# The identity and the causal tile of the mask products: fp32r copies in place of bf16 tiles

## The reference, cut to what matters

```python
x = L0_attn_a_x                                   # 2 x 512 tokens x 256
x = x + _L0_attn_a_ref(_layernorm(x), ...)        # block-sparse causal convolution
x = x + _L0_ffn_ref(_layernorm(x), ...)           # shared + 16 routed experts
x = x + _L0_attn_b_ref(_layernorm(x), ...)        # attention, below
x = x + _L0_ffn_ref(_layernorm(x), ...)

# inside _L0_attn_b_ref: 16 query heads of 128 in 4 key/value groups
scores = jnp.einsum('bhtd,bhsd->bhts', q, k) * scale
causal = jnp.tril(jnp.ones((t, t), dtype=bool))
scores = jnp.where(causal, scores, jnp.finfo(scores.dtype).min)
attn = jax.nn.softmax(scores, axis=-1)
out = jnp.einsum('bhts,bhsd->bhtd', attn, v)
```

## Time and profile before

| | |
|---|---|
| median of 3 runs | 873.85 us (873.17 to 874.07) |
| profiled execution, from first to last instruction (span) | 873.0 us |
| profiled execution, time of its own beside the span | not given apart; the fastest of the three runs took 873.17 us |
| TensorE busy (MATMUL) | 865.5 us, 99% |
| VectorE, ScalarE, GpSimd busy | 501.8, 420.0, 320.0 us |
| mask products (L1746) | 96, from 351.2 to 634.1 us of the span |

### The profile page before, as it was taken

The page is one execution under the profiler, slowest core; times in us unless marked ns, Lnnn a source line. Parts: engine busy times, 40 slices in busy tenths (PEclk is TensorE's granted clock), DMA queues, the critical chain, the costliest instruction groups (busy, mean ns, idle before and its releaser), DMA issues.

```text
span 873.0 us, 16737 instructions
## 1 busy us (share of the span) xinstructions
PE 865.5 (99%) x5617; PEld 773.3 (89%) x5620; DVE 501.8 (57%) x1360; ACT 420.0 (48%) x978; POOL 320.0 (37%) x293
## 2 busy tenths in 40 slices
PE   9999999999999999999999999999999999999998
PEld 7999878888888888889989998998997888888887
DVE  4777757333333338887688668768877433333334
ACT  3522416334334344776377557647746433434332
POOL 5211014556555564232121213212112556556552
PEclk9999999999999999999999999999999999999999
DMA  8999312111111102000000100000002111111111
GB/s 338 362 383 391 136 40 77 49 54 36 54 45 45 54 18 76 1 26 21 18 3 21 36 0 24 0 0 1 1 1 73 38 54 39 51 54 36 54 36 49
DMA packets 25554, 61.01 MB, mean 70 GB/s; under 512 B 3298, under 2 KB 10916, under 8 KB 25508
## 3 DMA queue, kind: packets, MB, share of 16 engines
q1 hardware_dynamic: 23204, 47.82, 16.1%
q0 software_dynamic: 2304, 12.58, 3.8%
HBM read 59.35 MB, written 1.05 MB: 69 GB/s over the span
## 4 chain that ended last, share of the span: by engine, by line
PE 93%; DVE 3%; ACT 1%; DMA 1%; issue 1%; POOL 0%; DVEq 0%; ACTq 0%
PE bank L1131 29%; PE bank L1655 25%; PE bank L1144 14%; PE bank L534 7%; PE bank L545 5%; PE bank L1781 4%; PE bank L1721 3%; PE bank L1157 2%; PE bank L1167 2%; DMA cv_shared<-in_wtaps 1%; PE bank L1746 1%; DVE cv_acc L421 1%; PE bank L518 1%; PE bank L1675 1%; PE bank L129 0%
## 5 line engine op out<-in xcount | busy, mean ns | idle before, releaser
L1030 DVE TENSOR_TENSOR f_h<-f_scaled,bank 128x512 f32<-128x512 f32 (+1 forms) x90 | 60.8, 676 | 179.4 <-POOL f_scaled L895 166.9
L812 ACT ACTIVATE f_h_hi<-f_h 128x512 fp32r<-128x512 f32 (+2 forms) x102 | 63.6, 624 | 186.2 <-DVE f_h L1030 186.0
L895 POOL TENSOR_TENSOR f_scaled<-f_act,f_gate_rows 128x512 f32<-128x512 f32 x80 | 102.9, 1287 | 116.3 <-ACT f_act L805 115.9
L1131 PE MATMUL bank<-f_xt_hi,f_w_lo 128*128 128x512 f32 x352 | 138.2, 393 | 0.0
L1131 PE MATMUL bank<-f_xt_hi,f_w_hi 128*128 128x512 f32 x352 | 137.8, 391 | 0.0
L1350 ACT ACTIVATE at_prob<-bank,at_sbias,at_qrs 128x512 f32<-128x512 f32 (+3 forms) x128 | 77.6, 618 | 72.6 <-DVE at_sbias L1542 72.6
L1037 DVE TENSOR_TENSOR f_h_lo<-f_h,f_h_hi 128x512 fp32r<-128x512 f32 (+2 forms) x102 | 71.8, 704 | 70.7 <-ACT f_h_hi L812 70.4
L1131 PE MATMUL bank<-f_xt_lo,f_w_hi 128*128 128x512 f32 x352 | 108.8, 390 | 0.0
L1144 PE MATMUL bank<-f_w_lo,f_h_hi 128*128 128x256 f32 (+1 forms) x352 | 99.6, 283 | 0.0
L1144 PE MATMUL bank<-f_w_hi,f_h_lo 128*128 128x256 f32 (+1 forms) x352 | 99.6, 283 | 0.0
L1144 PE MATMUL bank<-f_w_hi,f_h_hi 128*128 128x256 f32 (+1 forms) x352 | 99.3, 282 | 0.0
(11 more groups left out here) (232 smaller groups left out, 2062.8 us busy)
## 6 DMA issues: line engine op xcount, KB each, us to landing
cv_raw<-in_wconv SPq DMA_DIRECT2D x26, 512.0 KB, 6.7
cv_shared<-in_wtaps POOLq DMA_DIRECT2D x16, 768.0 KB, 7.7
f_wraw<-in_w SPq DMA_DIRECT2D x42, 256.0 KB, 2.6
xn<-in_wconv SPq DMA_DIRECT2D x14, 512.0 KB, 6.5
f_wraw<-in_w SPq DMA_DIRECT2D x42, 128.0 KB, 2.5
at_wraw<-in_wqkv SPq DMA_DIRECT2D x3, 768.0 KB, 4.4
at_oraw<-in_wo SPq DMA_DIRECT2D x4, 512.0 KB, 3.5
X<-in_x_tiles SPq DMA_DIRECT2D x2, 512.0 KB, 8.0
```

The source lines that it names most:

```text
L812: a.activation(h_hi[slot][0:rows, cols], h_f[half][0:rows, cols], ACT.Copy).then_inc(s["h_hi_done"], 1)
L895: g.tensor_tensor(scaled[half][:], act[half][:], gate_rows[:, half * HALF:(half + 1) * HALF], ALU.mult).then_inc(s["scaled_done"], 1)
L1030: v.tensor_tensor(h_f[half][0:rows, cols], src[half][0:rows, cols], pu[half][0:rows, cols], ALU.mult)\
L1131: mm = t.matmul((pg, pu)[gu][half][0:out_rows, :], w, x, start=q == 0, stop=q == 3 * KH - 1)
```

## The change

The bf16 identity is gone. Two new tiles, `ident_r` and `causal_r`, hold fp32r copies of `ident` and `causal`. ScalarE makes them with two activations late in the convolution phase, and TensorE waits once for them at the head of attention. The three mask products of each step use them in place of the bf16 tiles. The first feed-forward phase no longer allocates a semaphore that it did not use.

```diff
@@ conv_phase, scalar
                     round_sums(st, r)
+            for name in ("ident", "causal"):
+                a.activation(pm[f"{name}_r"][:], pm[name][:], ACT.Copy).then_inc(pm["masks_ready"], 1)
             first_weights["round"](a)
@@ conv_phase, gpsimd
             g.memset(pm["ident"][:], 0.0).then_inc(s["const_done"], 1)
-            g.memset(pm["ident_b"][:], 0.0).then_inc(s["const_done"], 1)
             g.memset(pm["causal"][:], 0.0).then_inc(s["const_done"], 1)
...
-            g.wait_ge(s["const_done"], 4)
-            for m in (pm["ident"], pm["ident_b"]):
-                g.affine_select(out=m[:], in_=m[:], compare_op=ALU.not_equal, fill=1.0, base=0,
-                                pattern=[[-1, P]], channel_multiplier=1)
+            g.wait_ge(s["const_done"], 3)
+            g.affine_select(out=pm["ident"][:], in_=pm["ident"][:], compare_op=ALU.not_equal, fill=1.0, base=0,
+                            pattern=[[-1, P]], channel_multiplier=1)
@@ ffn_phase
-            ... "x_added", "out_done")}
+            ... "x_added")
+             + (() if out is None else ("out_done",))}
@@ attention_phase, tensor, scores
-                        t.matmul(dst, pm["ident_b"][:], mask, start=True, stop=False, skip_group_check=True)
+                        t.matmul(dst, pm["ident_r"][:], mask, start=True, stop=False, skip_group_check=True)
...
-                    open_bank(diagonal(3), pm["causal"][:])
+                    open_bank(diagonal(3), pm["causal_r"][:])
...
-                            open_bank(diagonal(2), pm["causal"][:])
+                            open_bank(diagonal(2), pm["causal_r"][:])
...
-                                      pm["causal"][:].unsqueeze(1).to_broadcast([P, 2, P]))
+                                      pm["causal_r"][:].unsqueeze(1).to_broadcast([P, 2, P]))
@@ attention_phase, tensor
             ln["tensor"](t, 0)
+            t.wait_ge(pm["masks_ready"], 2)
             t.wait_ge(s["wkv_lo_done"], 1)
@@ build
-            "ident_b": sb("ident_b", [P, P], BF16),
             "causal": sb("causal", [P, P], BF16),
+            "ident_r": sb("ident_r", [P, P], F32R),
+            "causal_r": sb("causal_r", [P, P], F32R),
...
+        pm["masks_ready"] = cm("masks_ready")
```

More of the change, by code:

```diff
@@ L707, in ffn_phase @@
             "sentinels_ready", "gate_t", "gate_a", "gate_v", "comb_ready", "gate_rows_ready", "gu_ready", "act_done",
-            "last_w_in", "last_hi_done", "last_lo_done", "scaled_done", "h_ready", "h_hi_done", "h_lo_done", "down_done", "y_ready", "x_added", "out_done")}
+            "last_w_in", "last_hi_done", "last_lo_done", "scaled_done", "h_ready", "h_hi_done", "h_lo_done", "down_done", "y_ready", "x_added")
+             + (() if out is None else ("out_done",))}
         s["w13_hi_done"], s["w13_lo_done"] = first_weights["hi_done"], first_weights["lo_done"]
```

## The result

The changed kernel takes 877.58 us (median of five runs, 877.38 to 877.75), the kernel before 873.85 (873.17 to 874.19): 3.7 us more, ratio 1.004 with a 95% interval of 1.0028 to 1.0052. The forecast was 877.2, range 875.8 to 879.0.

The account below looks back on a forecast made before the run. TensorE's loads and products, one after the other, were taken to bound attention. 26 x 0.08 + 32 x 0.04 = 2.1 + 1.3 = 3.4 us on 873.85 gave 877.2 us, range 875.8 to 879.0, chance 0.80.

Parts of the forecast that it names:

- What bounds: Attention steps: TensorE's loads and products one after the other, no waiting; ordinary steps go from 7.40 to 7.52 us.
- Mask 1: Mask product after the query sums: its fp32r load costs 0.11 us against 0.03 for bf16, +0.08 us a step.
- Masks 2 and 3: Mask products behind a 512-column product: mask 2's load becomes hidden, mask 3's outlasts 128 columns, +0.04 us a step.
- How many steps pay: Attention: masks 2 and 3 pay in all 32 steps, mask 1 in 26, six waiting steps losing nothing for it.
- A: Rival: both costs vanish in unseen waits of a step; 875.5 us if in half the places, 873.9 if all; chance 0.08.
- B: Rival: changing between bf16 and fp32r itself costs time, so one kind throughout saves 2.9 us, 871.0; chance 0.04.
- C: Rival: mask 2's load isn't hidden, so masks 2 and 3 cost +0.15 us a step, 880.8 us; chance 0.06.
- D: Rival: each fp32r mask is issued as two passes, about 10.6 us more, 888 us; chance 0.02.
- The rest at nothing: Outside the masks: ScalarE copies, dropped GpSimd work and the new wait cost nothing; uncovered copies would cost 0.6 us once.
- 0.85 us around the span: Span 873.0 against the runs' median 873.85: 0.85 us lies around the span and the change leaves it alone.

Follow-up runs that it names:

- e7: Kernel before, with mask 3 (bf16) moved between the second and third query-sum products in steps 3 to 7 of a group only: 873.45 us, ratio 0.9993.
- e3: Changed kernel with all three masks back on bf16 tiles, the ScalarE copies, wait and fp32r tiles kept: 874.17 us, ratio 0.9999 to the kernel before.
- e1: Changed kernel with mask 1 alone back on the bf16 tiles: 875.32 us, ratio 1.0013 to the kernel before.
- e2: Changed kernel with masks 2 and 3 back on the bf16 tiles, mask 1 still fp32r: 875.75 us, ratio 1.0019 to the kernel before.
- e5: Kernel before with mask 1's bf16 product issued twice, the second writing the same values: 875.08 us, ratio 1.0013.

## Why the prediction was right

*What bounds.* TensorE without a gap, in the ordinary steps: right. The whole change of a step shows in the chain, 7.40 to 7.53, where 7.52 was forecast.

*Mask 1*, +0.08 in an ordinary step: +0.09 in the timeline. That it is the load was shown by putting it back and by doubling it. The quarter of the cycles that the prediction took from the Trainium skill ("TensorE: Matmul & The Clock Gate", Weight-path perf modes) stands there as the theory for fp8, beside about twice the speed as measured; here the bf16 load in the open took 0.03 us against 0.11, in e7 too.

*Masks 2 and 3*, +0.04: +0.05 in the timeline, and 0.03 when tried alone. The load for mask 2 became hidden as foreseen. What the hiding gives back is less than the load for mask 3 costs, which 128 columns don't cover.

*How many steps pay.* This step was off in its working, though the sum of attention came out near (3.2 us against 3.4). The prediction let the six waiting steps lose nothing for mask 1 and pay for masks 2 and 3. The opening of the second group shows more. Here are the second products of two successive steps on TensorE's timeline, before and then after, and the work of VectorE that the later step waits for ahead of its first product (the low part of the query), in the same order:

```profile
441.38 0.39 PE L1655 MATMUL bank<-at_kt_hi,at_qt_lo 128*128 128x512 f32 x1
...
449.09 0.39 PE L1655 MATMUL bank<-at_kt_hi,at_qt_lo 128*128 128x512 f32 x1
```

```profile
441.72 0.40 PE L1656 MATMUL bank<-at_kt_hi,at_qt_lo 128*128 128x512 f32 x1
...
449.35 0.39 PE L1656 MATMUL bank<-at_kt_hi,at_qt_lo 128*128 128x512 f32 x1
```

```profile
448.01 0.68 DVE L1497 TENSOR_TENSOR at_qt_lo<-bank,at_qt_hi 128x512 fp32r<-128x512 f32 x1
```

```profile
448.27 0.68 DVE L1498 TENSOR_TENSOR at_qt_lo<-bank,at_qt_hi 128x512 fp32r<-128x512 f32 x1
```

The distance falls from 7.71 to 7.63, where an ordinary step grows by 0.13. TensorE is 0.34 late in the first of the two steps and 0.26 in the second; VectorE is 0.25 to 0.26 late all the way, and had no pause from 440 to 445.8 in the kernel before, so it didn't see the delay of these masks. If masks 2 and 3 of the first step and mask 1 of the second were paid as in an ordinary step, TensorE would be 0.34 + 0.13 = 0.47 late in the second; it is 0.26. So the wait takes up 0.21 us: all three masks of the step ahead of it and mask 1 of its own, where the prediction let it take up that mask 1 alone, 0.08. In the first group, where three steps wait one after the other, the first three distances grow by 0.06 in all. In return the ordinary steps paid a little more than forecast (0.13 against 0.12). Over attention, the first error put the forecast about 0.5 us too high and the second about 0.3 too low. That they nearly cancel is luck.

*Rivals.* A (slack) holds at the openings alone. B (the change of kind costs time) is out: the kernels with both kinds in a step are faster than the one with fp32r alone, and in e7 a bf16 mask between two fp32 loads costs 0.03 us in all. C and D are out by the loads of the changed kernel: hidden, and one row each. (The text ahead of the prediction has all other stationary operands of attention as fp32 or fp32r. There are two bf16 loads of zeros, L59, in the opening of the first group at 355.3 us of the kernel before; they are no part of the change.)

*The rest at nothing.* Right: with copies, wait and tiles kept and the masks back on bf16, the time is that of before within 0.1%. The 3.7 us of the medians are 0.5 above the 3.2 in attention; that difference is within the spread of the runs (873.17 to 874.19 for the kernel before, a band of 1.0 us) and I have no other explanation for it. The prediction's 0.85 us around the span is a misreading: it set the span of one execution beside the median of others. In the executions whose time and span are both known it is 1.8 us (877.38 and 875.6 for the changed kernel, 874.17 and 872.4 for e3), so the profiled execution of the kernel before took about 874.8, by this estimate. The sum isn't touched, since the term stands on both sides of it.

## What to carry to other kernels

In this kernel a small fp32r product costs the longer of its weight load (0.11 us) and its stream (0.12 for 256 columns), so look at the load first when the type of a small stationary operand is changed: an identity in bf16 may be there for its short load, 0.03 us here where nothing hides it. A short load that isn't hidden is best put where the loads around it set the pace anyway. And before a product is moved to such a place, look for the wait that it carries, in the first rounds of a pipeline too and not in the steady ones alone.

## What the runs showed that I had not expected

A bf16 load costs 0.03 us among fp32 loads, and the 256 columns behind it nothing to 0.01 us; a second bf16 mask directly behind the first costs 0.06 among the loads and 0.04 in the step. Two products in a row with the same fp32r identity load it twice, 0.11 us each. The same instructions behind the masks took 0.01 us more a step in the kernel before than in the changed kernel, e1, e2 and e5 (6.27 against 6.26), which is a third of the smallest effect here.
